# Who multiplies the chunk states' input by its decay: the scalar engine instead of the vector engine

## What is computed

```python
A_cum = jnp.cumsum(A_dt, axis=-1)
Y_diag = jnp.einsum('bzlhn,bzshn,bhzls,bzshp->bzlhp', Cc, Bc, L, xch)
decay_states = jnp.exp(A_cum[..., -1:] - A_cum)
states = jnp.einsum('bzlhn,bhzl,bzlhp->bzhpn', Bc, decay_states, xch)   # states of each chunk
...
Y_off = jnp.einsum('bzlhn,bzhpn,bhzl->bzlhp', Cc, prev, jnp.exp(A_cum))
Y = (Y_diag + Y_off).reshape(b, s, H, P) + hs * D[None, None, :, None]
g = y * jax.nn.silu(gate)
...
return jnp.einsum('bsi,oi->bso', out, out_proj_w)
```

## Time and profile before

| | |
|---|---|
| median of three runs | 1723.99 us |
| the profiled execution | 1727.43 us (span 1726.1 us) |
| TensorE busy | 1596.4 us, 92% of the span |
| VectorE busy | 1536.7 us, 89% |
| GpSimd busy | 1378.2 us, 80% |
| ScalarE busy | 1237.4 us, 72% |
| mean granted TensorE clock | 0.985 |

### The profile page before, as it was taken

The page is one execution under the profiler, slowest core; times in us unless marked ns, Lnnn a source line. Parts: engine busy times, 40 slices in busy tenths (PEclk is TensorE's granted clock), DMA queues, the critical chain, the costliest instruction groups (busy, mean ns, idle before and its releaser), DMA issues.

```text
span 1726.1 us, 31398 instructions
## 1 busy us (share of the span) xinstructions
PE 1596.4 (92%) x10284; PEld 1259.0 (73%) x10284; DVE 1536.7 (89%) x1802; ACT 1237.4 (72%) x2625; POOL 1378.2 (80%) x1238
## 2 busy tenths in 40 slices
PE   7988999999989999899989999999999999989887
PEld 5777877777777777678767777777777777767675
DVE  5878889898998989999898989999898998989896
ACT  5277786777767787677867778677777777677773
POOL 3157698897889878897888979898788978888795
PEclk9999999999999999999999999999999999999998
DMA  3243476565645666546655556655655556554663
GB/s 122 75 178 115 134 189 196 165 157 158 185 142 154 163 166 184 136 124 169 190 165 162 140 153 187 170 141 160 180 157 139 149 153 182 181 140 133 170 186 92
DMA packets 289554, 269.41 MB, mean 156 GB/s; under 512 B 162408, under 2 KB 228976, under 8 KB 285168
## 3 DMA queue, kind: packets, MB, share of 16 engines
q1 hardware_dynamic: 289392, 267.40, 54.5%
HBM read 147.52 MB, written 55.05 MB: 117 GB/s over the span
## 4 chain that ended last, share of the span: by engine, by line
PE 34%; DVE 27%; issue 16%; POOL 11%; ACT 7%; DMA 3%; SPq 1%; DVEq 0%; ACTq 0%; POOLq 0%
DVE hsX L813 4%; PE P L280 4%; PE P L282 4%; PE P L281 4%; PE P L499 3%; PE P L489 3%; ACT P L602 3%; PE P L500 2%; PE P L506 2%; DVE yb L1079 2%; DVE P L1076 2%; PE P L364 2%; PE P L358 2%; PE P L357 2%; DVE OL L836 2%
## 5 line engine op out<-in xcount | busy, mean ns | idle before, releaser
L602 ACT ACTIVATE P<-AB,SC 128x128 f32<-128x128 f32 x1016 | 305.5, 358 | 0.0
L280 PE MATMUL P<-xh,AH 128*128 128x512 f32 x656 | 269.6, 411 | 29.7 <-DVE hsX L813 14.7
L282 PE MATMUL P<-xh,AL 128*128 128x512 f32 x656 | 260.1, 396 | 0.0
L281 PE MATMUL P<-xl,AH 128*128 128x512 f32 x656 | 260.0, 396 | 0.0
L813 DVE SCALAR_TENSOR_TENSOR hsX<-P,cwt,hsX 128x1023 f32<-128x1023 f32 x189 | 241.6, 1279 | 19.4 <-ACT hsX L539 15.0
L774 ACT ACTIVATE sq<-yb 128x512 bf16<-128x512 f32 x128 | 80.8, 632 | 230.5 <-DVE yb L1079 230.4
L1122 POOL TENSOR_TENSOR AL<-AR,AH 128x512 fp32r<-128x512 f32 x82 | 121.4, 1481 | 144.7 <-ACT AH L526 144.6
L499 PE MATMUL P<-OH,gTh 128*128 128x512 f32 x512 | 217.0, 424 | 10.6 <-issue 5.1
L357 PE MATMUL P<-GH,xh 128*128 128x512 f32 x512 | 201.5, 394 | 2.3 <-ACT GH L571 2.3
L500 PE MATMUL P<-OH,gTl 128*128 128x512 f32 x512 | 202.5, 396 | 0.0
L883 DVE TENSOR_TENSOR EM<-P,Gt 128x1024 f32<-128x1024 f32 x127 | 153.5, 1209 | 53.5 <-ACT P L607 30.5
(11 more groups left out here) (219 smaller groups left out, 4149.1 us busy)
## 6 DMA issues: line engine op xcount, KB each, us to landing
AB<-acr_d SPq DMA_DIRECT2D x128, 512.0 KB, 4.8
half_d<-hsX SPq DMA_DIRECT2D x60, 512.0 KB, 3.4
AR<-in_wa SPq DMA_DIRECT2D x80, 256.0 KB, 2.7
TS<-in_wg SPq DMA_DIRECT2D x16, 1024.0 KB, 5.6
TS<-in_wo SPq DMA_DIRECT2D x16, 1024.0 KB, 7.8
al<-al SPq DMA_DIRECT2D x256, 64.0 KB, 2.2
part_d<-pl SPq DMA_DIRECT2D x64, 256.0 KB, 3.1
pl<-part_d SPq DMA_DIRECT2D x64, 256.0 KB, 3.2
```

The lines of the kernel that those rows point to most:

```text
L280: te.matmul(o, ah_, bh_, start=(first and i == 0), stop=False)
L281: te.matmul(o, ah_, bl_, start=False, stop=False)
L282: r = te.matmul(o, al_, bh_, start=False, stop=(last and i == n - 1))
L602: r = se.activation(decays(m)[:, h, :], AB[m % 2][:, h, :], ACT.Relu, bias=SC[s % 2][:, c, 3, h:h + 1], scale=-1.0)
```

## The change

`dve_scaled` goes, with its call ahead of the loop and the one in each slot. `act_scaled` comes in its place and is called in `act_state_hi`, after `SH` and ahead of `DH`. It makes the same product with eight ACTIVATE instructions, one per head, each of 128 x 64, whose scale is a column of `SC` (one number per partition). The waits are those of `dve_scaled`, and one on `s_dh`, which ACT itself raises. Nothing else is changed.

```diff
+        def act_scaled(m):
+            s, c = divmod(m, 8)
+            if s:
+                se.wait_ge(ht_in[m % 2], 16 * (m // 2 - 3))
+            else:
+                se.wait_ge(s_hsr, m + 1)
+            se.wait_ge(sc_in[s % 2], 32 * (s // 2 + 1))
+            if m:
+                se.wait_ge(s_dl, n7(m) - 1)
+                se.wait_ge(s_dh, n7(m) - 1)
+            for h in range(8):
+                d = slice(h * 64, h * 64 + 64)
+                r = se.activation(dxh[:, d], HT[m % 2][:, d], ACT.Copy, scale=SC[s % 2][:, c, 2, h:h + 1])
+            r.then_inc(s_dxh, 1)
+
         def act_state_hi(m):
...
             if m % 8 != 7:
+                act_scaled(m)
                 se.wait_ge(s_dxh, n7(m))
...
-        def dve_scaled(m):
...
-            if c != 7:
-                if m:
-                    ve.wait_ge(s_dl, n7(m) - 1)
-                ve.tensor_tensor(h8(dxh[:, :]), h8(HT[m % 2]), bc(SC[s % 2][:, c, 2, :]), ALU.mult).then_inc(s_dxh, 1)
...
             dve_blocks(0)
-            dve_scaled(0)
             dve_decay(0)
...
                     if c == out_c:
                         dve_output_lo(s, (0,))
-                    dve_scaled(m + 1)
```

## The result

Three runs of the changed kernel gave 1680.16, 1680.53 and 1682.38 us, a median of 1680.53 us against 1723.99 us: a ratio of 0.975 with a 95% interval of 0.972 to 0.977, 43.5 us less. The span of the profiled execution fell from 1726.1 to 1681.1 us, by 45.0. The sign was forecast, the size was not: the forecast was 1704 us and its range ended at 1688.

A forecast was written before the change was run, and what follows sets the result against it. No single engine was taken as the bound: time was a sum of slots limited by TensorE, VectorE or ScalarE. Terms -20.4, -3.5, -3.5, +6.3 and +1.3 gave -19.8 us, so a median of 1704 us, range 1688 to 1738.

The forecast's parts named there:

- (d): Even stages, c = 0: square 1.7 us late, exponential about 1.2 us late, so VectorE enters c = 2 1.2 us late.
- (e): Slots 72 and 73: ScalarE's delay makes tg 0.3 to 1.0 us late; 0.9 us booked 7 times, 6.3 us lost.
- (a): Odd stages 1 to 13, c = 3 and 4: VectorE full, ScalarE idle; 1.46 us gained per slot, 20.4 us in all.
- (c): Odd stages, c = 7: GpSimd's L1249 no longer waits beside VectorE's L871; 0.5 us gained 7 times, 3.5 us.
- (f): Slots 119 to 121: ScalarE 2.3 us late, VectorE gets up to 2.7 us back behind them; 1.3 us loss booked.
- (b): Even stages, c = 2: at most 0.95 us can come out, limited by ScalarE's tap; 1.5 us in stage 0.
- (g): GpSimd stands about 1 us because DL waits for the later DH; nothing booked, 21 us as a bound.
- ScalarE as the bound: Rival: ScalarE's missing idle time goes straight into the slots, 1749 us, or 1739 if half the odd-stage gain stays; chance 0.20.
- No change: Rival: next instruction takes up the wait, only 0.68 us goes, GpSimd's stall eats that: 1722 us; 1715 to 1730 has 0.24.
- The gain comes out whole: Rival: ScalarE's delays are taken in by waits not seen, 31 us gained, 1693 us; 1680 to 1695 has chance 0.14.
- the train of 2.0 us: Sign on ScalarE: 896 new instructions, their train of eight near 2.0 us; 2.6 us or more would refute the prediction.
- `DL` behind `DH`: Sign on GpSimd: DL waits for DH in most slots.

The follow-up runs named there:

- e5: Kernel before, with ScalarE making the product only for chunks 4 and 5 of odd stages 1 to 13 (14 of 112 calls): 1691.84 us, ratio 0.981.
- e7: Changed kernel, but VectorE makes the product for chunk 1 of the odd stages and the last stage's first three chunks: 1679.62 us, ratio 0.974.
- e8: Changed kernel, but VectorE makes the product for chunks 1 and 2 of the odd stages and the last stage's first three: 1679.28 us, ratio 0.973.
- e3: Kernel before, VectorE keeping its product, with the eight ACTIVATEs added on ScalarE into a tile nobody reads: 1741.27 us, ratio 1.010.
- e1: Changed kernel with the product left out on every engine, DH and DL made from HT itself: 1671.14 us, ratio 0.970 against the kernel before.
- e4: Kernel before, with dummy matmuls ahead of three long waits of TensorE in the odd stages: 1713.95 us, ratio 0.995.
- e11: Product on ScalarE only for odd-stage chunks 4, 5 and even-stage chunks 0, 3, none in the last stage, plus dummy matmuls: 1677.60 us, ratio 0.973.
- e10: Changed kernel, but ScalarE makes the product only for odd-stage chunks 4, 5 and even-stage chunks 0, 3, none in the last stage: 1677.54 us, ratio 0.972.

## Why the prediction was wrong

Two steps failed. The forecast booked ScalarE's delays in (d) and (e) nearly in full, where the runs show that most of them end in other waits: about 8 us. And it put TensorE's clock at nothing without saying so, where before loses 11 us to it behind its stops. Another 3 to 4 us lie in two stages with a wait for a DMA. (a), (c) and (f) came to the sum that was booked.

Term by term, from the intervals between TensorE's markers. "Pattern" is what all stages share. The clock is what the single intervals of before with a half-clock stretch have beyond the others: five times 1.6 us in c = 7, 3.0 us in c = 4 and 5. The waits for a DMA are those in two stages only.

| term | predicted | measured |
|---|---|---|
| (a) odd c = 3, 4 | -20.4 | -22 (7 x (0.7 + 2.4)) |
| (b), (d) even stages and stage 0 | -3.5 | -6 (7 x -0.90, +0.2) |
| (c) odd c = 7 | -3.5 | -3 (7 x 0.4) |
| (e) slots 72, 73 (c = 0, 1, 2) | +6.3 | +1 (7 x (-0.25 + 0.95 - 0.58)) |
| (f) last stage | +1.3 | +2 |
| (g) stall of GpSimd | 0 | 0 |
| small remainders | | -1 |
| the pattern | -19.8 | -29 to -30 |
| TensorE's clock | not a term | -11 |
| waits for a DMA in two stages | not a term | -3 to -4 |

**(a), right in sum, wrong in its halves.** 2.9 us a pair were forecast, 3.1 came. But in after slot 75 gives 0.84 us (14.26 to 13.42) and slot 76 gives 2.29 (15.19 to 12.90), not 1.46 each. The premise that the stand behind GpSimd passes to the next instruction held (`silu` took 2.31 and 2.12 us, 2.06 before). What was not looked at is who stands behind whom at `gTl`, one instruction earlier: in slot 76 it turned for the better, as in e5, and in slot 75 of after for the worse (`gTl` 1.42 us, 0.81 before; by TensorE's markers the halves are 0.7 and 2.4):

```profile
1048.34 1.29 POOL L1124 TENSOR_TENSOR AL<-AR,AH 128x512 fp32r<-128x512 f32 x1
...
1048.76 1.42 DVE L1116 TENSOR_TENSOR gTl<-gtd,gTh 128x512 fp32r<-128x512 f32 x1
...
1050.10 2.31 DVE L858 SCALAR_TENSOR_TENSOR hsX<-th,hsX 128x1024 f32<-128x1024 f32 x1
```

**(d), the step that failed among the delays.** The price of a call was right (its 307 ns is 308 in the row, which changes nothing): the train of eight takes 2.01 us, and `DH` starts 2.57 us behind `SH` (929.28 to 931.85 in slot 65) instead of 0.52, 2.05 us more against 2.1 forecast. The delay of ScalarE in slot 64 was right too: the square starts 922.48 - 914.87 = 7.61 us behind the `Y` matmuls, 946.41 - 940.42 = 5.99 before, so 1.6 us late, 1.7 forecast. What failed is where it goes. By the same marker the exponential of slot 65 starts 0.8 us later than before, VectorE's first sum 0.5 us later, not 1.2, and `tg` of that slot not later at all: it waited 1.85 us for TensorE before and waits 0.41 now. The rows of after, slots 65 and 66:

```profile
929.46 1.22 DVE L887 TENSOR_TENSOR EM<-P,Gt 128x1024 f32<-128x1024 f32 x1 [1.40 <-ACT P L607]
...
934.11 0.60 ACT L793 ACTIVATE tg<-P 128x512 f32<-128x512 f32 x1 [0.41 <-PE P L364]
...
942.37 3.92 DVE L829 SCALAR_TENSOR_TENSOR hsX<-P,cwt,hsX 128x1023 f32<-128x1023 f32 x3 [0.75 <-ACT hsX L539]
```

The convolution starts at 942.37 - 914.87 = 27.50 us, against 968.88 - 940.42 = 28.46 before: 0.96 us earlier, the whole of the 0.95 us that (b) allowed, with VectorE now waiting for ScalarE's tap. The forecast had stopped its reading at the exponential and not gone on to the wait of `tg`, which takes ScalarE's lateness in wherever TensorE is what `tg` waits for.

**(e), mis-sized in the same way.** 0.9 us a pair were booked, 0.95 came in c = 1, and 0.8 of it is given back in c = 0 and c = 2; e7 and e8 show that undoing the cause moves it back and forth with no change in the sum. VectorE waits more for the exponential of slot 73 (1.40 us before):

```profile
1028.01 1.22 DVE L887 TENSOR_TENSOR EM<-P,Gt 128x1024 f32<-128x1024 f32 x1 [2.25 <-ACT P L607]
```

but VectorE, relieved of its product in slots 72 and 74, seems to have the time to wait. I had charged ScalarE's delays at the full and given VectorE nothing back in the slots around them. e3 shows a price like the one that I had in mind, 17 us with the clock's part in it, when VectorE keeps its work, and after against e1 a smaller one, 9 us.

**(c) and (f)** came as booked, within a microsecond. **(g)** was left out, and nothing shows that it cost: `DL` waits 74.7 us for `DH` in all, and in e3, where it waits 86.6, the odd stages are only 1.0 us longer with everything in it. No run tests it by itself; it is part of the 9 us that e1 gives for all of the new work.

**The clock was no term at all,** and it is the largest miss: 11 us of 24. The forecast said that TensorE waits 1.79 us ahead of L469 and booked the shorter wait as time won once. A shorter stop can also keep the clock up, and so win a second time in the matmuls behind it. That there was something to win could have been read from before: its mean granted clock was 0.985, and a view by short windows shows the seven stretches.

**The rest,** 3 to 4 us, is in c = 2 of stages 11 and 13 (16.8 us before, 15.06 and 14.35 after). It goes with a wait of VectorE's transpose for a DMA just ahead of it, twice in before, 1.69 us here and 1.90 at 1464.35:

```profile
1258.97 1.09 DVE L1084 STREAM_TRANSPOSE al<-yb 128x512 f32<-128x512 f32 x1 [1.69 <-DMA al<-al]
```

After has the same two waits, 1.89 us at 1229.16 and 1.08 in stage 13, and eleven of the thirteen traces have the one in stage 11; only in e4 (2.01 us, stage 5) and e11 do such waits stand elsewhere. So the wait itself did not go; what changed is what it costs. The traces divide by who makes the product of chunk 3 of the odd stages, in slot c = 2 right behind the wait: VectorE in before, e3, e4, e5, e10 and e11, and each has an interval c = 2 of 16.7 us or more; ScalarE in the seven others (nobody in e1), where none is above 15.1. That suggests that the 3 to 4 us belong to the change. What sets the waits, and how the product adds to them, was not tested and stays open.

**The rivals.** ScalarE as the bound is true only of chunks 112 to 127. "No change" had rightly seen that the stand passes to the next instruction, and wrongly that this eats the gain. "The gain comes out whole", 1693 us, was the right mechanism for (d) and (e); with the clock's 11 us it would have been 1682, and the runs gave 1680.5. Of the signs named ahead, the train of 2.0 us, the busy times (1449.6 for about 1470, 1424.2 for about 1420), the square's idle time under 100 us, the 2.9 us of slots 75 to 77 (3.06) and `DL` behind `DH` (89 times) came true. TensorE's waits in slots 75 to 77 did not all but go: they fell from 3.5 to 1.0 us. And "slots 68 to 72 as long as before" is true only by TensorE's markers. The waits for the exponential grew by 28 us, 20 forecast, and yet cost hardly anything. (The Trainium skill, "Perfetto Trace Analysis", section "Optimizing Scalar/DVE Operations", says that where VectorE is saturated, moving some of its work to ScalarE may make sense, although VectorE is the faster one where it has a performance mode. The runs agree on the first half, with a limit: e10 has the full gain with 30 of the 112 moves.)

## What to carry to other kernels

Cost a move slot by slot, and follow a delay on the receiving engine up to the next place where it waited for a third engine before: here ScalarE's `tg` waited 1.85 us for TensorE, and a delay of 1.6 us ended there. When a change shortens TensorE's stops, look up the granted clock in the windows behind them: here a stretch at half clock cost 1.5 to 1.6 us of its own, and six of seven went when only the stops were shortened (e4). Measure slots by the engine that the change does not touch; a marker on an engine that gets work moves by itself.

## What was not expected of the hardware

Where two engines meet at the same time, which comes first decides: with `AL` 0.09 us ahead, `gTl` takes 1.75 us; 0.07 us behind, 0.67 us, and `AL` then takes 1.76 instead of 1.30. A shift of 0.2 us moved 1.1 us from one engine to the other.

Useless matmuls can make a kernel faster: 94 of them took 10.4 us off (e4), since TensorE's stops before them had been followed by matmuls 0.43 us apart instead of 0.23.

Why the clock holds in after at 911 us behind a stop of 1.50 us, and fell in before at 935 behind one of 1.59, the rows settle only in part. The two stops ahead of it were longer in before (1.79 and 1.10 us, against 1.03 and 1.03), but that is not what it takes: in stage 13 of e4 they were 0.43 and 0.19 us, and the clock fell all the same behind the stop of 1.59. Nor does such a stop suffice: in e5 the seven of them, 1.58 to 1.60 us each, were followed by three falls, and in before the same seven by five.
